# A state-space layer and a mixture of experts on one core: two weights' transfers move from ScalarE's queue to SyncE's, one wait is loosened, and the written order of all five engines is laid anew

## What is computed

```
n = layernorm(x);  u, res = split(n @ W_in);  u = silu(u)
delta = softplus(u @ W_delta + b);  B = u @ W_B;  C = u @ W_C
h[p] = exp(delta * A) * h[p-1] + delta * B * u        (16 states per channel)
y = (sum over states of h * C + u * D) * silu(res);  x1 = x + y @ W_out
```

## Time and profile before

| | |
|---|---|
| median of three runs | 1491.57 us |
| the profiled execution | 1491.69 us, of which 1489.9 us are the span of its instructions |
| busy | PE 1407.7 us (94%), DVE 1308.3 (88%), ACT 1227.8 (82%), POOL 1184.7 (80%) |
| table loads on ACT | 321, mean 1283 ns |
| the longest in the chain of waits | PE 57%, ACT 15%, DVE 11%, issue 11%, POOL 3% |

### The profile page before, as it was taken

How to read it: one execution, slowest core, us unless ns; L and a number is a source line. 1 busy time by engine, 2 the same in 40 slices (tenths; PEclk the granted TensorE clock), 3 DMA queues, 4 the chain that set the end, 5 groups by cost and what they waited for, 6 DMA issues and landing times.

```text
span 1489.9 us, 28303 instructions
## 1 busy us (share of the span) xinstructions
PE 1407.7 (94%) x8950; PEld 1170.4 (79%) x8950; DVE 1308.3 (88%) x2444; ACT 1227.8 (82%) x1759; POOL 1184.7 (80%) x655
## 2 busy tenths in 40 slices
...
DMA packets 88218, 146.40 MB, mean 98 GB/s; under 512 B 11305, under 2 KB 42790, under 8 KB 88070
## 3 DMA queue, kind: packets, MB, share of 16 engines
...
...
## 4 chain that ended last, share of the span: by engine, by line
PE 57%; ACT 15%; DVE 11%; issue 11%; POOL 3%; DMA 1%; ACTq 1%; DVEq 0%; SPq 0%; POOLq 0%
PE eo_bank L1306 14%; PE turn L1240 9%; PE shared L1292 9%; PE shared L1294 8%; PE shared L1293 8%; DVE hb L1052 6%; ACT L894 6%; ACT decay L977 3%; DVE acc L1064 3%; PE shared L1197 2%; POOL hb L841 2%; ACT s L987 2%; PE shared L1205 2%; DVE gated L1134 1%; PE eo_bank L1251 1%
## 5 line engine op out<-in xcount | busy, mean ns | idle before, releaser
L841 POOL TENSOR_TENSOR hb<-soft,bbc 128x1024 f32<-128x1024 f32 x256 | 605.4, 2384 | 42.3 <-PE turn L1240 41.0
L1052 DVE TENSOR_TENSOR_SCAN hb<-decay,hb 128x512 f32<-128x512 f32 x512 | 606.2, 1210 | 36.2 <-ACT decay L977 21.2
L894 ACT ACT_TABLE_LOAD x321 | 411.8, 1283 | 5.9
L1306 PEld LDWEIGHTS eo_bank<-w_sb,gated 128*128 128x128 f32 x3072 | 383.1, 192 | 31.0 <-issue 11.3
L1306 PE MATMUL eo_bank<-w_sb,gated 128*128 128x128 f32 x3072 | 399.5, 276 | 4.4 <-POOL gated L870 4.3
L977 ACT ACTIVATE decay<-delta,a_sb 128x510 f32<-128x510 f32 x512 | 342.5, 686 | 69.3 <-DVE hb L1052 65.0
L1064 DVE SCALAR_TENSOR_TENSOR acc<-turn,c_sb,acc 128x256 f32<-128x256 f32 x900 | 378.8, 473 | 18.0 <-PE turn L1240 16.1
L870 POOL TENSOR_TENSOR gated<-gated,wb 128x1024 f32<-128x1024 f32 x128 | 304.4, 2382 | 87.1 <-DVE gated L1134 65.1
L1240 PE MATMUL turn<-ident,hb 128*128 128x128 f32 x2048 | 299.6, 278 | 23.1 <-DVE acc L1064 15.3
L1134 DVE TENSOR_TENSOR gated<-shared,s 128x512 f32<-128x512 f32 x384 | 257.5, 680 | 62.0 <-PE shared L1294 43.0
L987 ACT ACTIVATE s<-shared 128x512 f32<-128x512 f32 x384 | 218.2, 597 | 111.5 <-PE shared L1294 84.7
...
## 6 DMA issues: line engine op xcount, KB each, us to landing
bbc<-b_rows SPq DMA_DIRECT2D x128, 512.0 KB, 4.9
wb<-w_rows SPq DMA_DIRECT2D x128, 256.0 KB, 7.0
...
x_in<-x_dram SPq DMA_DIRECT2D x16, 256.0 KB, 2.9
x_cur<-x_dram SPq DMA_DIRECT2D x16, 256.0 KB, 2.8
...
out_dram<-o SPq DMA_DIRECT2D x15, 256.0 KB, 2.3
```

The source lines that it names most:

```text
L841: pool.tensor_tensor(hb[:, arg % HB_RING, :, :], du[:, h, :].unsqueeze(1).broadcast_to((P, GN, TOK)), bbc[:, r, :].rearrange("p (n t) -> p ...
L894: act.preload_act_table_set(table)
L1052: dve.tensor_tensor_scan(states, decay_bank[i][:, :], states, 0.0, ALU.mult, ALU.add)\
L1306: mm = pe.matmul(eo_bank[:, blk * P:(blk + 1) * P], gated[:, k % GATED_RING, blk * P:(blk + 1) * P], w3_sb[:, k, :], start=(arg == 0 and k ...
```

## The change

Three things change. W1's and W2's 12 transfers are issued by SP, right behind the small weights that it issues after the first `load_x`. `ud` of tile t waits for the output projection of tile t-1 on PE (`wo` in PSUM) and no longer for `x1` on DVE. And all five orders are laid anew: they hold the same entries as before, each exactly once, in another sequence. Counted in the texts, ACT changes its table 315 times instead of 321. In the order of SP, the last broadcast of a tile, `bbc.7`, stands behind the `w_out` of the tile before in six tiles (1, 4, 7, 8, 12 and 13); it did in none before.

```
 SP_ORDER = """
-0:load_x.0 0:load_cur.0 1:load_x.0 0:b_out.0 0:bbc.0.1.2.3 2:load_x.0 0:bbc.4 1:b_out.0 0:bbc.5.6.7 1:bbc.0.1.2.3
...
+0:load_x.0 1:load_x.0 0:b_out.0 0:bbc.0.1.2.3 1:b_out.0 0:bbc.4.5.6 2:load_x.0 0:bbc.7 1:bbc.0 0:load_cur.0 1:bbc.1.2
...
+3:load_cur.0 1:store.0 4:bbc.4 2:wbc.8.9.10 4:bbc.5.6 3:w_out.0 4:bbc.7 7:load_x.0 3:wbc.0.1 5:b_out.0 3:wbc.2
...
 ACT_ORDER = """
-0:xn.0 0:xT.0 0:wi.0.1 0:wi_res.0.1 0:ud.0.1 0:zb.0.1 0:bt.0 0:soft.0 1:xn.0 0:decay1.0 0:decay0.0 1:xT.0 1:wi.0.1
...
-0:prod.25.26 2:xn.0 0:prod.27 0:decay1.15 0:prod.28.29.30.31 1:wi_res.0.1 1:zb.0.1 1:soft.0 1:ud.0.1 0:x1n.0 2:xT.0
...
+0:xn.0 0:xT.0 0:wi.0.1 0:wi_res.0 0:ud.0.1 0:zb.0 0:wi_res.1 0:zb.1 0:bt.0 0:soft.0 1:xn.0 1:xT.0 0:decay1.0
...
+0:prod.25 0:decay0.15 0:prod.26.27 0:decay1.15 0:prod.28.29.30.31 2:xn.0 1:wi_res.0.1 1:zb.0.1 1:soft.0 2:xT.0 1:ud.0
+0:x1n.0 1:ud.1 1:decay0.0 0:x1T.0 1:decay1.0 0:xh.0 2:wi.0.1 3:xn.0 1:decay0.1 1:decay1.1 1:decay0.2 1:decay1.2
...
 DVE_ORDER = """
-0:ln.0 0:split.0.1 1:ln.0 0:c.0 0:scan0.0 0:scan1.0 2:ln.0 0:scan0.1 0:scan1.1 0:scan0.2 0:scan1.2 0:scan0.3 0:scan1.3
...
+0:ln.0 1:ln.0 0:c.0 0:split.0.1 0:scan0.0 0:scan1.0 0:scan0.1 0:scan1.1 0:scan0.2 0:scan1.2 0:scan0.3 0:scan1.3
...
+            def load_w1_w2():
+
+                sp_eng.wait_ge(blank, 2)
+                for dst, src, landed in ((stage, w1_all, w1_in), (stage2, w2_all, w2_in)):
...
+                        sp_eng.dma_start(by_group[:, grp, 0:GROUP * WHOLE].rearrange("p (i c) -> p i c", i=GROUP),
+                                         src_of[:, grp, :, 0:WHOLE]).then_inc(landed, 16)
+                        sp_eng.dma_start(by_group[:, grp, GROUP * WHOLE:GROUP * HID].rearrange("p (i c) -> p i c", i=GROUP),
+                                         src_of[:, grp, :, WHOLE:]).then_inc(landed, 16)
...
                         if t == 0:
                             load_small()
+                            load_w1_w2()
...
                         act.wait_ge(wi_ready, NH * t + arg + 1)
-                        wait_if(act, x1_ready, t)
+                        wait_if(act, full["wo"], t)
...
             act.activation(a_sb[:, :, :], a_sb[:, :, :], ACT.Exp).then_inc(a_exped, 1)
-            act.wait_ge(blank, 2)
-            for dst, src, landed in ((stage, w1_all, w1_in), (stage2, w2_all, w2_in)):
...
-                    act.dma_start(by_group[:, grp, 0:GROUP * WHOLE].rearrange("p (i c) -> p i c", i=GROUP),
-                                  src_of[:, grp, :, 0:WHOLE]).then_inc(landed, 16)
...
             act.wait_ge(consts, CONSTS)
```

More of the change, by code:

```diff
@@ L86 @@
[L86 to L95, removed]
@@ new lines @@
+1:gated.16 3:scan1.4 3:scan0.4 1:gated.17 3:sum.2 3:scan1.5 3:sum.3 1:gated.18 3:sum.4 3:scan0.5 3:scan1.6 3:sum.5
+1:gated.19 3:sum.6.7 3:scan0.6 3:scan1.7 3:scan0.7 3:sum.8 1:gated.20 2:x1.0 3:scan1.8 2:x1s.0 3:sum.9.10
+1:gated.21.22 3:sum.11 3:scan0.8 3:scan1.9 1:gated.23 3:scan0.9 2:xl.0 2:ga.0 3:scan1.10 2:gb.0 2:gc.0 3:sum.12 2:gd.0
+3:scan0.10 1:out.0 2:gated.0 3:sum.13 3:scan1.11 2:gated.1 2:ginv.0 6:ln.0 2:gated.2 3:sum.14.15 3:scan1.12 2:gated.3
+3:scan0.11 3:sum.16 2:gated.4 3:scan0.12 3:scan1.13 3:scan0.13 3:scan1.14 3:scan0.14 3:sum.17.18 2:gated.5 3:sum.19.20
@@ new lines @@
+3:ga.0 3:xl.0 4:scan1.10 3:gb.0 3:gc.0 3:gd.0 4:sum.11 3:ginv.0 4:sum.12 4:scan0.10 3:gated.0.1 4:scan1.11 4:sum.13
+2:out.0 4:sum.14 3:gated.2 4:scan0.11 4:sum.15 4:scan1.12 4:sum.16 3:gated.3.4 4:scan0.12 4:scan1.13 4:scan0.13
+4:scan1.14 4:scan0.14 7:ln.0 3:gated.5 4:scan0.15 4:sum.17.18.19.20.21.22 3:gated.6 4:scan1.15 3:gated.7 4:sum.23.24
+3:gated.8 4:sum.25.26 5:scan1.0 3:gated.9 5:scan0.0 4:sum.27 5:scan0.1 3:gated.10.11 5:scan1.1 4:sum.28 5:scan0.2
+3:gated.12.13 4:sum.29.30 5:scan0.3 5:scan1.2 3:gated.14.15 4:sum.31 5:scan1.3 4:z.0 5:scan0.4 4:z.1 5:c.0 3:gated.16
@@ new lines @@
+5:scan1.4 5:scan0.5 3:gated.17 5:scan1.5 5:sum.2.3 3:gated.18 5:scan0.6 5:sum.4.5 3:gated.19 5:sum.6 5:scan1.6
+5:scan0.7 4:x1.0 5:scan1.7 5:sum.7 3:gated.20 5:sum.8 4:x1s.0 5:scan1.8 5:sum.9 3:gated.21 5:sum.10 5:scan0.8
+5:scan1.9 3:gated.22.23 5:scan0.9 5:scan1.10 4:ga.0 4:gb.0 4:xl.0 4:gc.0 5:sum.11 4:gd.0 5:sum.12 5:scan0.10
+5:scan1.11 8:ln.0 4:ginv.0 4:gated.0.1 5:sum.13 3:out.0 5:scan0.11 5:scan1.12 4:gated.2 5:sum.14 4:gated.3 5:scan0.12
+5:sum.15 5:scan1.13 4:gated.4 5:sum.16 5:scan0.13 5:scan1.14 5:scan0.14 4:gated.5 5:sum.17.18 5:scan1.15
@@ new lines @@
+5:ga.0 6:scan1.10 5:gb.0 6:sum.11 5:gc.0 5:xl.0 5:gd.0 6:scan0.10 6:scan1.11 9:ln.0 5:ginv.0 6:sum.12 5:gated.0
+4:out.0 5:gated.1 6:sum.13 6:scan0.11 6:scan1.12 5:gated.2 6:sum.14.15 5:gated.3.4 6:scan0.12 6:scan1.13 6:scan0.13
+6:scan1.14 6:scan0.14 5:gated.5 6:sum.16.17.18 6:scan0.15 6:sum.19 6:scan1.15 6:sum.20.21.22 5:gated.6 6:sum.23
+5:gated.7 6:sum.24 5:gated.8 6:sum.25 7:scan1.0 7:scan0.0 5:gated.9.10 6:sum.26.27 7:scan0.1 7:scan1.1 5:gated.11
+6:sum.28 5:gated.12 6:sum.29 7:scan0.2 7:scan1.2 6:sum.30 5:gated.13 6:sum.31 5:gated.14 7:scan1.3 7:scan0.3
@@ new lines @@
+8:scan0.9 7:ga.0 8:scan1.10 7:gb.0 7:xl.0 7:gc.0 7:gd.0 8:sum.12 7:ginv.0 6:out.0 7:gated.0 8:sum.13 7:gated.1 11:ln.0
+8:scan1.11 8:scan0.10 7:gated.2.3 8:scan0.11 8:sum.14.15 8:scan1.12 8:sum.16 7:gated.4 8:scan0.12 8:scan1.13
+8:scan0.13 8:scan1.14 8:scan0.14 8:sum.17.18 7:gated.5 8:sum.19.20 8:scan1.15 8:sum.21.22 8:scan0.15 8:sum.23
+7:gated.6 8:sum.24.25 7:gated.7.8 8:sum.26 9:scan0.0 9:scan1.0 8:sum.27 7:gated.9.10 8:sum.28 9:scan0.1 9:scan1.1
+7:gated.11.12 9:scan1.2 9:scan0.2 8:sum.29.30 7:gated.13 9:scan1.3 7:gated.14 9:scan0.3 7:gated.15.16 8:sum.31
@@ new lines @@
+9:scan0.4 9:scan1.4 9:c.0 7:gated.17 8:z.0.1 9:scan0.5 9:scan1.5 9:sum.2 9:scan0.6 9:sum.3 9:scan1.6 9:sum.4.5.6
+7:gated.18 9:sum.7 9:scan0.7 8:x1.0 7:gated.19 8:x1s.0 7:gated.20 9:scan1.7 9:scan0.8 9:sum.8 7:gated.21 9:sum.9.10
+7:gated.22 9:scan1.8 9:scan0.9 9:scan1.9 8:xl.0 8:ga.0 7:gated.23 9:scan1.10 8:gb.0 9:sum.11 8:gc.0 8:gd.0 9:scan1.11
+9:sum.12 8:gated.0 9:scan0.10 9:sum.13.14 7:out.0 12:ln.0 8:ginv.0 8:gated.1 9:scan1.12 8:gated.2 9:scan0.11 9:sum.15
+8:gated.3 9:scan0.12 9:sum.16 9:scan1.13 8:gated.4 9:scan0.13 9:scan1.14 9:scan0.14 9:sum.17 8:gated.5 9:sum.18
@@ new lines @@
+10:sum.11 10:scan0.8 8:gated.22.23 10:scan1.9 10:scan0.9 9:ga.0 9:xl.0 9:gb.0 10:scan1.10 9:gc.0 9:gd.0 10:sum.12
+9:ginv.0 10:scan0.10 13:ln.0 9:gated.0.1 10:sum.13.14 10:scan1.11 10:sum.15 8:out.0 9:gated.2.3.4 10:scan1.12
+10:scan0.11 10:sum.16 9:gated.5 10:scan0.12 10:scan1.13 10:scan0.13 10:scan1.14 10:scan0.14 10:scan1.15 10:scan0.15
+10:sum.17.18.19.20.21.22.23.24 9:gated.6.7 10:sum.25.26 9:gated.8 11:scan1.0 11:scan0.0 10:sum.27 9:gated.9 10:sum.28
+9:gated.10 11:scan0.1 10:sum.29 11:scan1.1 10:sum.30 9:gated.11 11:scan1.2 11:scan0.2 9:gated.12.13 10:sum.31
@@ new lines @@
+11:scan1.3 11:scan0.3 9:gated.14.15 11:scan0.4 10:z.0 11:scan1.4 10:z.1 11:c.0 9:gated.16 11:scan1.5 11:scan0.5
+9:gated.17 11:sum.2.3 11:scan0.6 11:sum.4 11:scan1.6 11:sum.5 9:gated.18.19 11:sum.6 11:scan1.7 11:scan0.7 9:gated.20
+11:sum.7 10:x1.0 11:scan1.8 10:x1s.0 11:sum.8 9:gated.21 11:scan0.8 9:gated.22 11:sum.9.10 9:gated.23 11:sum.11
+11:scan1.9 11:scan0.9 10:ga.0 10:gb.0 11:scan1.10 10:gc.0 10:xl.0 10:gd.0 11:sum.12.13 11:scan1.11 11:scan0.10
+10:ginv.0 10:gated.0 11:sum.14 9:out.0 10:gated.1.2 11:scan0.11 14:ln.0 11:scan1.12 10:gated.3 11:sum.15 10:gated.4
@@ new lines @@
+12:sum.8 11:x1.0 12:sum.9 10:gated.19 12:scan0.7 12:sum.10 10:gated.20 11:x1s.0 12:scan1.8 10:gated.21 12:scan0.8
+10:gated.22 12:sum.11 12:scan1.9 10:gated.23 12:scan0.9 12:scan1.10 11:ga.0 11:gb.0 11:gc.0 11:xl.0 11:gd.0
+12:scan0.10 11:ginv.0 10:out.0 11:gated.0 12:sum.12.13 12:scan1.11 11:gated.1 15:ln.0 11:gated.2.3 12:sum.14
+12:scan0.11 11:gated.4 12:sum.15.16 12:scan1.12 12:scan0.12 12:scan1.13 12:scan0.13 12:scan1.14 12:scan0.14 11:gated.5
+12:sum.17.18.19 12:scan1.15 12:sum.20.21.22 12:scan0.15 11:gated.6 12:sum.23 11:gated.7 12:sum.24.25 11:gated.8
@@ new lines @@
+12:gc.0 12:gd.0 13:sum.11 13:scan0.10 13:sum.12 12:gated.0.1 12:ginv.0 13:sum.13 13:scan1.11 11:out.0 12:gated.2
+13:sum.14 12:gated.3 13:sum.15 13:scan1.12 13:scan0.11 13:sum.16 12:gated.4 13:scan0.12 13:scan1.13 13:scan0.13
+13:scan1.14 13:scan0.14 13:sum.17 12:gated.5 13:sum.18.19 13:scan1.15 13:sum.20.21 13:scan0.15 13:sum.22.23 12:gated.6
+13:sum.24 12:gated.7.8 13:sum.25 14:scan0.0 14:scan1.0 13:sum.26 12:gated.9 13:sum.27 12:gated.10 13:sum.28 14:scan0.1
+12:gated.11 14:scan1.1 12:gated.12 13:sum.29 14:scan0.2 12:gated.13 13:sum.30 14:scan0.3 12:gated.14 14:scan1.2
```

748 lines of the change are left out of this document (372 added, 376 removed).

## The result

The changed kernel takes 1480.08 us (median of 4 runs, 1478.91 to 1482.30), the kernel before 1491.05 beside it (1489.93 to 1492.17): ratio 0.9928, 95% interval 0.9911 to 0.9945, so 11 us or 0.7% less. The profiled execution took 1480.54. The forecast was 1477 and the range 1463 to 1490; the size is right, but the profile shows at once that it did not come about as forecast.

A forecast was written before the change was run, and what follows sets the result against it. No engine waits long in the middle: DVE is busy 949 of 1000 us, PE 974, ACT 881, and DVE has at most 51 us to give. 1491.69 - 7.5 - 1 - 6 = 1477.2, said as 1477; range 1463 to 1490.

The forecast's parts named there:

- The orders laid anew: All five engine queues: same entries interleaved differently, six fewer ACT table loads; nothing counted, bounded at 0.6 us per tile, 8 us.
- Rival C: SP's queue, six tiles: bbc.7 behind w_out comes late; if its cover fails, 22 us lost, 1505; chance 0.12.
- Its mark in my list: Sign of being wrong: POOL's dbu waiting for the transfer of bbc in tiles 4, 7, 8, 12 and 13.
- The start: Tile 0: W1 and W2 issued by SP let xn start earlier; first scan about 32.0 instead of 39.90, -7.5 us.
- my list of signs of being wrong: First scan after 35; dbu waiting for bbc; DVE's busy share below 949 in 300 to 1300 with longer scan waits.
- now they begin at 20.4 and the shift ends at 23.5: Tile 1's layernorm: statistics on DVE begin at 20.4 instead of 24.65, POOL's shift ends at 23.5 instead of 27.72.
- ud: ACT, 300 to 1300 us: its 17.4 us wait for x1 loosened; half of the scans' 11.7 us decay wait returns, -6.
- xn of tile 2: ACT, tile 0: moved behind the prod entries, where a 4.06 us wait hides its 1.65 us; -1 us.
- Rivals A: Only the start gains; DVE keeps the middle at 86.6 us per tile; 1483, between 1480 and 1487; chance 0.22.
- B: Every stall of ud turns into pace, all 17.4 us come back; 1466; chance 0.12.
- D: The 12 issues block SP as long as ACT; first scan at 39, no gain at the start; 1485; chance 0.06.

## Why the prediction held in size and not in its steps

The ledger, from one run to the next:

| step | us |
|---|---|
| before, beside both edits | 1490.5 |
| both edits, old orders | 1476.6 (-13.9) |
| new orders of PE, ACT, DVE and POOL, split first, new places of load_cur and store on SP | 1442.1 (-34.6) |
| b_out and bbc on SP as changed | 1477.1 (+35.1) |
| split behind c: the changed kernel | 1480.1 (+3.0) |

**The orders laid anew** are the step that failed: "The rest is a different interleaving. Bound from both sides: 0.6 us per tile, worth 8 us over 13 tiles, is as far as I let it go". Two large terms stand there, -34.6 and +35.1, each four times that bound; that they cancel is why 1477 came near, and that is luck. It is luck a second time that the two named edits, forecast at -7.5 and -6, gave -5.7 and -10.4 alone and -13.9 together: their errors went opposite ways. I had bounded one number where five queues had been laid anew, and those can be off in opposite directions. The two terms go by this one path: SP's new order under the old orders of the other four engines was not run.

**Rival C** had the mechanism (a broadcast behind an entry of SP's queue that waits) and a price of 22 us, but only one of its places. For bbc 7 behind w_out I found cover of 3.9 us at the scan and called it hidden; moving those of five tiles (and five more entries) gave 2.2 us, so that was about right. Tile 1's gave 5.4, and the largest part, 27 us (1469.4 to 1442.1), lies in the rest, which I had not followed: some 9 at tile 12, where bbc 2 to 5 stand behind a wbc, the others not traced one by one. Its mark in my list, dbu waiting for bbc, was there, but mostly marked "issue", also where the transfer had been issued and not yet landed (tile 12: issued from 1034.49, dbu 4 at 1045.86).

**The start**, forecast at -7.5: xn and split came about as worked out, softplus 2.5 us sooner still, and the first scan missed by 6 us; it began after 35, which stood on my list of signs of being wrong. "now they begin at 20.4 and the shift ends at 23.5" is where it broke: I took 3.1 us for the statistics and the small operations from a stretch where DVE was doing nothing large, and put them beside split. By itself the edit is worth 5.7 us; the changed kernel has 1.6 of it at the first scan, though there it costs 8.0 to take the edit back.

By the Trainium skill, page "SBUF — State Buffer", section "Who interferes with whom", VectorE and GpSimd share one pair of ports under an exclusive lock: a cast of VectorE in certain modes holds the pair for the whole instruction, and a VectorE operation with two inputs in SBUF contends with a GpSimd operation that reads SBUF. For split the trace agrees: each POOL operation waited for the end of one of DVE's (0.20 us became 2.49). For the scans, which have two such inputs too, it doesn't: in the changed kernel they took 1.20 to 1.23 us and POOL's 256 dbu 2.34 to 2.46, side by side. I had not weighed the rule, and it spoke against the new DVE order.

**ud**, forecast at -6: -10.4 alone. The mechanism was right, the size was not: I counted only decays as the way from ACT's lateness to DVE, and left out the silus, PE and gated.

**xn of tile 2**, forecast at -1: alone, in the old orders, it costs 3.9 us, since I had not asked what its end releases. In the changed kernel its share can't be told apart.

**Rivals A, B and D** fall: the middle did get faster (85.5 us per tile), and not by all of ud's wait. D's time for the first scan (39) came near the 38.31 measured, but not by its mechanism: x of tile 1 was there at 19.62, ahead of the 20.4 I had worked out.

What stays open: which of the four engines' new orders carries the 34.6 us, which of b_out and bbc the 35.1, and whether the start could win more with delta ahead of tile 1's layernorm on POOL; none of these was tried.
